# Products of a constant bf16 tile in 25 gaps of TensorE, in a fused four-layer network on one core

## The chip, the cores and the metric

One core of one Trainium2 chip runs one program. Its engines work side by side, each through its own list of instructions, and meet only at semaphores and barriers: TensorE (PE: matmuls and PE-mode transposes; PEld is its loading of weights), VectorE (DVE), ScalarE (ACT), GpSimd (POOL) and SyncE (SP, which issues most DMAs). The metric is the device time of one execution in microseconds (us), lower is better, as the median of several runs.

TensorE's clock has two levels here, 1.2 and 2.4 GHz. The profile shows what was granted as a share of the higher one: 0.50 is 1.2 GHz and 1.00 is 2.4 GHz.

## The reference

The residual stream x is [4, 256, 256] in float32, 1024 rows of 256. Four layers follow one another; each is an attention and a feed-forward part ("ffn"), each behind a layernorm and scaled by tanh of a gate:

```python
x = x + jnp.tanh(g_xattn[0]) * _L0_xattn_ref(_layernorm(x), ctx_512, ...)
x = x + jnp.tanh(g_ffn[0])   * _L0_ffn_ref(_layernorm(x), ...)
...
x = x + jnp.tanh(g_xattn[3]) * _L3_xattn_ref(_layernorm(x), ctx_512, ...)
x = x + jnp.tanh(g_ffn[3])   * _L3_ffn_ref(_layernorm(x), ...)
return x
```

What the parts compute:

```python
# layers 0 and 1: latent attention, 16 heads of 128, 64 latents per sequence (rope on
# the keys; in layer 0 on the queries too)
q_big  = jnp.einsum('bshk,hkq->bshq', (x @ Wq.T).reshape(B, S, H, K), w_kc_q)
scores = jnp.einsum('bhsr,bhlr->bhsl', q_r, k_r)
ctx_c  = jnp.einsum('bhsl,bld->bhsd', softmax(scores), kv_r)
out    = jnp.einsum('bhsd,hkd->bhsk', ctx_c, w_kc_kv) -> [B, S, H*K] @ Wo.T
# layers 2 and 3: causal attention with 16 heads of 16
scores = where(tril, q k^T / 4, min);  out = (softmax(scores) v) @ Wout.T
# ffn 0: top 6 of 16 experts (width 176) and one shared expert (width 352), silu gating
# ffn 1: w1, w2 made ternary by their mean size; gelu(x @ w1q.T + b1) @ w2q.T + b2
# ffn 2: rows of x and of the weight rounded to int8, one product, scaled back, + bias
# ffn 3: top 2 of 8 experts (width 512) and one shared expert, silu gating
```

## The kernel before

The whole stream stays in on-chip memory (tile X, 128 partitions by 8 token tiles of 256). The work is written out as a row of blocks, one for each part of a layer. A block lists each engine's instructions by hand; at its end all engines meet in a barrier, which each reaches only when its own work has drained. So no engine can start a part before the slowest of the part before has ended. Within a block the order on each engine is fixed by the code, and semaphores pass tiles between engines.

The blocks in order, with the stretch of the profiled span that they take:

- attn0, two blocks. The first (0 to 174 us, called `latent_rope` in the code) goes over 8 pairs of heads. Before the loop TensorE makes the first pair's query weights (`query_weights(0, True)`) and turns the first half of the normalised input with PE transposes (`turn_rows`); after the loop it turns the last two pairs' probabilities (`turn(NP - 2)`, `turn(NP - 1)`, line 680). The second block (to 215 us, `latent_out`) projects to the output.
- ffn0 (215 to 464 us, tiles `ffn_...`, lines 2174 and on): transposes, router logits, a count of the chosen rows, the list of rows for each of 63 work items (`index()`, line 2491), then the 63 items. Each item begins with a gather of its rows by GpSimd's indirect DMA (line 2220); TensorE turns them (line 2518) and multiplies (lines 2510, 2541).
- chain1 (465 to 519 us): the weights of layer 1's attention are folded; at its end TensorE transposes the normalised stream (line 222, the helper `normalise`).
- attn1 (519 to 594 us), ffn1 (594 to 642 us), attn2 (642 to 711 us), ffn2 (711 to 735 us), attn3 (735 to 804 us). attn2 and attn3 run the same code (`plain_attend`): projections, then a loop over 8 token tiles with `turn` (line 1219), `context` (line 1230), `turn_context` (line 1238) and `project` (line 1244).
- ffn3 (804 us to the end): 16 transposes (line 1962), 32 router products of 8 columns (line 1970), then the shared expert in 8 items and the routed ones in 23 (`up` line 1994, `down` line 2021, `turn_h` line 2011).

Most float32 products are made of three: the helper `mm3` (lines 95 to 97) multiplies high and low halves of both operands in the type fp32r. ffn0's and ffn3's experts use plain float32. A "transpose" is a product with the identity.

## Time and profile before

| what | value |
|---|---|
| median of 3 runs (lowest, highest) | 1020.25 us (1019.51, 1020.53) |
| profiled execution, its own time | 1013.3 us |
| span of its instructions | 1011.5 us |
| mean granted TensorE clock over the span | 0.924 |
| TensorE busy | 887.4 us, 88% of the span |
| VectorE, GpSimd, ScalarE busy | 569.6, 424.9, 345.8 us |
| DMA | 84.81 MB, mean 84 GB/s |

The stretches in which the profile grants half the clock are, in us from the span's start: 167 to 181, 215 to 232, 236 to 239, 253 to 270, 468 to 471, 505 to 522, 584 to 587, 594 to 604, 642 to 649, 662 to 666, 707 to 727, 731 to 744, 754 to 758, 802 to 819, and from 1007 on. Clock records begin at 20.6 us; ahead of that the page shows full clock for want of a record.

How to read the rows further down: a timeline row has the start of an instruction (or of a run of equal ones, with their count behind the x), the time it took, its engine, its line in the kernel, the tile written and the tiles read, and in brackets how long the engine had idled before it and what released it. "PEq" or "SPq" there is an engine's sequencer, which is what a barrier looks like.

### The profile page before, as it was taken

To read this page: it belongs to the slowest core of one execution; us is meant where nothing else is said; L and a number is where in the kernel's file an instruction comes from. 1 tells how busy PE (TensorE), PEld (TensorE's weight loads), DVE (VectorE), ACT (ScalarE), POOL (GpSimd) and SP (SyncE) were. 2 spreads that over 40 slices of the span, in tenths; PEclk is the share of its full clock that TensorE was granted. 3 is DMA by queue.
4 is the path that set the end of the run, shared out by engine and by line. 5 is a ranking of instruction groups with operands and counts; after the bars stand their busy time and mean duration, and the time that the engine had idled before them with its cause. 6 is when DMAs were issued, how large, how long until landed. Compare 5 with 4: busy or idle time off the path is not lost. (4 is left out here: it accounts for less than half of the span.)

```text
span 1011.5 us, 14571 instructions
## 1 busy us (share of the span) xinstructions
PE 887.4 (88%) x4711; PEld 690.1 (68%) x4711; DVE 569.6 (56%) x1068; ACT 345.8 (34%) x612; POOL 424.9 (42%) x341
## 2 busy tenths in 40 slices
PE   4999995988699999999859978897389799999996
PEld 3899995986466666667649966776278665566564
DVE  5788886549344344443578977667767532222221
ACT  3454543311133333333425436333143421122111
POOL 5787883030388888674402230630360006122222
PEclk9999998978699999999969979899579879999999
DMA  8321110039445435756520010100000194322210
GB/s 304 128 78 56 45 44 1 1 123 409 132 81 85 79 69 87 149 74 177 155 84 1 1 37 1 38 1 1 11 0 1 51 427 172 86 45 43 36 30 11
DMA packets 38593, 84.81 MB, mean 84 GB/s; under 512 B 9741, under 2 KB 27533, under 8 KB 36014
## 3 DMA queue, kind: packets, MB, share of 16 engines
q1 hardware_dynamic: 22062, 64.56, 18.1%
q0 software_dynamic: 16176, 19.31, 11.5%
q8 instruction: 39, 0.64, 0.3%
q14 instruction: 28, 0.23, 0.1%
q10 hardware_dynamic: 288, 0.07, 0.0%
HBM read 71.23 MB, written 20.68 MB: 91 GB/s over the span
## 5 line engine op out<-in xcount | busy, mean ns | idle before, releaser
L2510 PE MATMUL ffn_GU<-ffn_W,ffn_XTB 128*128 x252 | 91.2, 484 | 1.9 <-DVE ffn_XTB L2418 1.3
L1994 PE MATMUL ffn_GU<-ffn_W,ffn_XTB 128*128 x184 | 85.0, 604 | 0.0
L2220 POOL DMA_INDIRECT kept_MARKED<-scratch_rows,kept_IDX x63 | 62.4, 990 | 51.5 <-DMA scratch_rows<-ffn_WEIGHT 32.6
L1815 POOL DMA_INDIRECT out_x<-ffn_YB,ffn_XB x23 | 35.8, 1557 | 113.5 <-DVE ffn_YB L1943 92.3
L2402 DVE TENSOR_TENSOR ffn_GB<-ffn_GU,ffn_BIAS 128x352 f32<-128x352 f32 x63 | 33.0, 524 | 88.2 <-PE ffn_GU L2510 88.2
L2510 PEld LDWEIGHTS ffn_GU<-ffn_W,ffn_XTB 128*128 128x128 f32 x252 | 43.7, 191 | 34.3 <-issue 20.1
L2541 PE MATMUL ffn_DN<-ffn_W,ffn_HT 96*128 x252 | 64.8, 379 | 0.0
L2258 ACT ACTIVATE ffn_HG<-ffn_GB 128x176 f32<-128x176 f32 x63 | 22.1, 350 | 115.6 <-DVE ffn_GB L2402 115.6
L2021 PE MATMUL ffn_DN<-ffn_W,ffn_HT 128*128 (+1 forms) x248 | 58.7, 380 | 0.8 <-ACT ffn_HT L1838 0.8
L1932 DVE COPY ffn_XTB<-ffn_XP 128x256 f32<-128x256 f32 x23 | 9.8, 424 | 87.6 <-PE ffn_XP L2003 87.6
L1994 PEld LDWEIGHTS ffn_GU<-ffn_W,ffn_XTB 128*128 128x128 f32 x184 | 33.1, 189 | 36.0 <-issue 33.7
L348 POOL TENSOR_TENSOR attn_RP<-attn_RP,attn_RS 128x512 f32<-128x512 f32 x32 | 40.6, 1291 | 34.3 <-DVE attn_RS L515 34.3
L2021 PEld LDWEIGHTS ffn_DN<-ffn_W,ffn_HT 128*128 128x128 f32 x248 | 45.2, 190 | 9.2 <-issue 4.4
L1832 ACT ACTIVATE ffn_HG<-ffn_GU 128x512 f32<-128x512 f32 x31 | 18.5, 597 | 90.9 <-PE ffn_GU L1994 90.9
L2541 PEld LDWEIGHTS ffn_DN<-ffn_W,ffn_HT 96*128 96x128 f32 x252 | 43.0, 190 | 3.5
L343 POOL TENSOR_TENSOR attn_WS_lo<-attn_W,attn_WS_hi 128x896 fp32r<-128x896 f32 (+2 forms) x24 | 41.4, 1742 | 5.4 <-ACT attn_WS_hi L419 5.4
L95 PE MATMUL attn_QB<-attn_XT_hi,attn_C_hi 128*128 128x512 f32 x96 | 39.2, 408 | 3.0 <-DVE attn_XT_lo L557 3.0
L1062 POOL TENSOR_TENSOR attn_PROB<-XN,attn_SM 128x1024 f32<-128x1024 f32 x8 | 15.2, 1904 | 62.6 <-DVE attn_SM L1085 62.6
L97 PE MATMUL attn_QB<-attn_XT_hi,attn_C_lo 128*128 128x512 f32 x96 | 38.0, 396 | 0.0
L96 PE MATMUL attn_QB<-attn_XT_lo,attn_C_hi 128*128 128x512 f32 x96 | 38.0, 396 | 0.0
L1838 ACT ACTIVATE ffn_HT<-ffn_HP 128x512 f32<-128x512 f32 x31 | 18.5, 597 | 55.1 <-PE ffn_HP L2011 55.1
L1926 DVE TENSOR_TENSOR ffn_HF<-ffn_GU,ffn_HG 128x512 f32<-128x512 f32 x31 | 21.4, 691 | 25.9 <-ACT ffn_HG L1832 25.8
(506 smaller groups left out, 2471.3 us busy)
## 6 DMA issues: line engine op xcount, KB each, us to landing
ffn_W<-in_f_w SPq DMA_DIRECT2D x9, 1536.0 KB, 19.3
ffn_W<-in_f_w SPq DMA_DIRECT2D x16, 608.0 KB, 17.6
attn_W<-in_L_pairs SPq DMA_DIRECT2D x7, 1088.0 KB, 4.9
scratch_rows<-in_rows_empty SPq DMA_DIRECT2D x1, 2967.0 KB, 13.3
ffn_XB<-scratch_rows SPq DMA_DIRECT2D x23, 129.0 KB, 2.1
ffn_BIAS<-in_f_bias SPq DMA_DIRECT2D x1, 2816.0 KB, 16.4
kept_STAGE<-in_f_w SPq DMA_DIRECT2D x1, 2048.0 KB, 7.9
kept_STAGE<-in_L_pairs SPq DMA_DIRECT2D x2, 768.0 KB, 9.1
```

The lines of the kernel that those rows point to most:

```text
L95: pe.matmul(out, a[0], b[0], start=first, stop=False)
L96: pe.matmul(out, a[0], b[1], start=False, stop=False)
L97: return pe.matmul(out, a[1], b[0], start=False, stop=last)
L343: pool.tensor_tensor(WS[1][:, SECTIONS[c]], W[:, SECTIONS[c]], WS[0][:, SECTIONS[c]].bitcast(F32), ALU.subtract).then_inc(w_lo[c], 1)
L348: pool.tensor_tensor(RP[:, q, g, :], RP[:, q, g, :], RS[:, g, 1 - q, :], ALU.add).then_inc(rope_add, 1)
L1815: pool.indirect_dma_start(out[:, :], bass.IndirectOffsetOnAxis(ap=XB[:, i % NB, D:D + 1].bitcast(I32), axis=0), YB[:, i % 3, :], None, bou ...
L1994: last = pe.matmul(GU[:, m, :], x, weights(e, k * 2 * HID3 + m * HID3, HID3), start=k == 0, stop=k == KD - 1)
L2021: last = pe.matmul(DN[:, n % 2, 0:D], HT[:, n % 2, c * P:(c + 1) * P], weights(e, UPW + c * D, D), start=c == 0, stop=c == HID3 // P - 1)
L2220: pool.indirect_dma_start(XB[:, i % NB, :], None, DR["rows0"][:, :], bass.IndirectOffsetOnAxis(ap=IDX[:, i:i + 1], axis=0)).then_inc(rows_ ...
L2402: dve.tensor_tensor(GB[:, n % 2, :], GU[:, n % 2, 0:2 * HID], BIAS[:, bass.ds(e * (2 * HID), 2 * HID)], ALU.add).then_inc(biased, 1)
L2510: last = pe.matmul(GU[:, n % 2, 0:2 * HID], XTB[:, i % 2, k * P:(k + 1) * P], flat[:, bass.ds(e * WIDTH0 + k * 2 * HID, 2 * HID)], start=k ...
L2541: last = pe.matmul(DN[:, n % 2, 0:D], HT[0:rows, n % 2, j * P:(j + 1) * P], w, start=j == 0, stop=j == len(parts) - 1)
```

## The change

A tile WARM of 128 by 512 bf16 values is added and set to 1.0 by VectorE, as its first memset. A helper `keep_busy(pe, bank, n)` issues n products of WARM's first 128 columns with all of WARM into a PSUM bank that nobody reads at that point. Nothing else is computed with it. It is called at 25 places, 311 products in all. The numbers, in program order: attn0 9, 18, 4, 24 and 7; its second block 7; ffn0 5, 7 and 32; chain1 46; attn1 6 and 5; ffn1 8, 6, 8 and 14; attn2 8, 8 and 5; ffn2 24, 12 and 20; attn3 8, 8 and 12. ffn3 gets none. Three waits come with them: PE waits for the memset before the first group, in chain1 for 14 of 16 halves before the 46, and in ffn2 for one step of scaling before the 20. In attn1 the wait for the eighth shift stands ahead of the 6.

```diff
         MASK = sbuf(top, "CAUSAL", [P, L], BF16)
+        WARM = sbuf(top, "WARM", [P, 512], BF16)
...
             xt[:] = split(ctx, "XT", [P, KD, B * S])
+
+        def keep_busy(pe, bank, n):
+
+            for _ in range(n):
+                pe.matmul(bank, WARM[:, 0:P], WARM[:, :], start=True, stop=True)
...
-            def tensor(pe):
+            def tensor(pe, between=None):
                 for j in range(4):
+                    if j == 2 and between:
+                        between()
                     if j // 2 >= normalised:
...
                 x_in = [sem(ctx, f"x_in_{h}") for h in range(2)]
-                consts_set, mask_steps, gates_done, kvb_cleared = (sem(ctx, s) for s in ("consts_set", "mask_steps", "gates_done", "kvb_cleared"))
+                consts_set, mask_steps, gates_done, kvb_cleared, warm_set = (sem(ctx, s) for s in ("consts_set", "mask_steps", "gates_done", "kvb_cleared", "warm_set"))
                 rope, kvb_ready = Count(sem(ctx, "rope_steps")), sem(ctx, "kvb_ready")
...
+                        dve.memset(WARM[:, :], 1.0).then_inc(warm_set, 1)
                         for part in KVB:
...
+                        pe.wait_ge(warm_set, 1)
+                        keep_busy(pe, TR[:, 1, :], 9)
                         query_weights(0, True)
+                        keep_busy(pe, TR[:, 1, :], 18)
                         turn_rows(0)
                         turn_rows(1)
+                        keep_busy(pe, TR[:, 1, :], 4)
...
                         turn(NP - 2, False)
+                        keep_busy(pe, QB[:, 0, :], 24)
                         turn(NP - 1, False)
+                        keep_busy(pe, QB[:, 0, :], 7)
...
                                 last.then_inc(out_ps, 1)
+                        keep_busy(pe, ZP[:, 0, :], 7)
...
                             step(g)
+                        pe.wait_ge(g_lo, 4 * ROUNDS - 2)
+                        keep_busy(pe, GB[:, 0, :], 46)
                         pe.wait_ge(g_lo, 4 * ROUNDS)
...
                                 value(2 * i)
+                            if i == T:
+                                pe.wait_ge(shifted, T)
+                                keep_busy(pe, SC[:, 0, :], 6)
                             if 1 <= i <= T:
...
                                 mix(i - 2)
+                        keep_busy(pe, SC[:, 0, :], 5)
...
                         score(1)
+                        keep_busy(pe, TR[:, 0, :], 8)
                         for i in range(1, STEPS):
...
                                 turn(i - 1)
+                            if i == STEPS - 1:
+                                keep_busy(pe, TR[:, 0, :], 8)
                             if i >= 2:
...
                                 context(i - 1)
+                        keep_busy(pe, TR[:, 0, :], 5 if following else 12)
...
                         pe.matmul(UP[:, 0, 0:2], ONES[:, :], ASUM[:, 1:4:2], start=False, stop=True).then_inc(mean_ps, 1)
-                        nrm["tensor"](pe)
+                        nrm["tensor"](pe, lambda: keep_busy(pe, UP[:, 3, :], 8))
+                        keep_busy(pe, UP[:, 3, :], 6)
...
                                 pe.wait_ge(nrm["ready"], 4)
+                                keep_busy(pe, NB[:, 3, :], 8)
                             pe.wait_ge(h_lo, NF * (t // 4 + 1))
...
                                 up(n)
+                        keep_busy(pe, UP[:, 0, :], 14)
...
                         last.then_inc(wt_ps, 1)
+                        keep_busy(pe, OP[:, 0, :], 24)
                         turn_tokens(0)
+                        keep_busy(pe, OP[:, 0, :], 12)
                         turn_tokens(1)
...
                             last.then_inc(out_ps, 1)
+                        pe.wait_ge(scaled_steps, 1)
+                        keep_busy(pe, SP[:, :], 20)
...
                         for j in range(4):
+                            if j == 2:
+                                keep_busy(pe, RL[:, :], 5)
                             if j // 2 == 1:
...
                         def count():
+                            keep_busy(pe, RL[:, :], 7)
                             pe.wait_ge(chosen, 1)
...
                         index()
+                        keep_busy(pe, XP[:, :], 32)
                         pe.wait_ge(w_in, 16 * E)
```

Line numbers of the changed kernel are higher than those of the one before, by 9 near the start and by 33 in ffn3. Its order of instructions shows the new products as rows of line 153. Three places follow.

TensorE at the start of attn0; the rows of attn_WS are the query weights of pair 0, the row with IDENT is `turn_rows(0)` and `turn_rows(1)`. Before:

```order
L97 MATMUL attn_QB<-attn_WS_hi,attn_WS_lo 128x192
L603 MATMUL attn_QB<-IDENT,XN 128x128 x8
L95 MATMUL attn_QB<-attn_XT_hi,attn_C_hi 128x512
L96 MATMUL attn_QB<-attn_XT_lo,attn_C_hi 128x512
L97 MATMUL attn_QB<-attn_XT_hi,attn_C_lo 128x512
```

And in the changed kernel:

```order
L97 MATMUL attn_QB<-attn_WS_hi,attn_WS_lo 128x192
L153 MATMUL attn_TR<-WARM 128x512 x18
L612 MATMUL attn_QB<-IDENT,XN 128x128 x8
L153 MATMUL attn_TR<-WARM 128x512 x4
L95 MATMUL attn_QB<-attn_XT_hi,attn_C_hi 128x512
L96 MATMUL attn_QB<-attn_XT_lo,attn_C_hi 128x512
L97 MATMUL attn_QB<-attn_XT_hi,attn_C_lo 128x512
```

Eighteen products now stand between the weights and the transposes, and four between the transposes and the queries.

TensorE in ffn0, from the last step of `index()` to the first item (the row with ffn_TURNED ends the index, TENSOR_LOAD reads the item's expert number, the row with kept_MARKED turns the gathered rows), in the changed kernel:

```order
L2523 MATMUL ffn_RA<-IDENT,ffn_OWN 1x128
L2527 MATMUL ffn_RL<-ffn_TURNED 128x63
L153 MATMUL ffn_XP<-WARM 128x512 x32
L2581 TENSOR_LOAD ffn_EI
L2581 ISA x2
L2554 MATMUL ffn_XP<-IDENT,kept_MARKED 128x128 x2
```

Only the row of WARM is new; the 32 products stand ahead of the load and of the wait for the gathered rows.

TensorE at the end of attn3 (attn_CT is `context`, attn_OP<-IDENT is `turn_context`, the next row `project`, the branches are the block's end, and the last row is the first of ffn3). Before:

```order
L1230 MATMUL attn_CT<-kept_VB,attn_AT 128x34 x8
L1238 MATMUL attn_OP<-IDENT,attn_CN 128x128 x2
L1244 MATMUL attn_OP<-ffn_QO,attn_CTS 128x256 x2
L1162 UNCONDITIONAL_BRANCH
L1956 UNCONDITIONAL_BRANCH
L1962 MATMUL ffn_GU<-IDENT,ffn_XE 128x128 x8
```

And in the changed kernel:

```order
L1252 MATMUL attn_CT<-kept_VB,attn_AT 128x34 x8
L153 MATMUL attn_TR<-WARM 128x512 x8
L1260 MATMUL attn_OP<-IDENT,attn_CN 128x128 x2
L1266 MATMUL attn_OP<-ffn_QO,attn_CTS 128x256 x2
L153 MATMUL attn_TR<-WARM 128x512 x12
L1184 UNCONDITIONAL_BRANCH
L1989 UNCONDITIONAL_BRANCH
L1995 MATMUL ffn_GU<-IDENT,ffn_XE 128x128 x8
```

Eight products now stand between the last context and its transposes, and twelve between the last projection and the barrier.

## Rows read from the trace of the kernel before

**Rows 1.** TensorE's timeline, 0 to 24 us: start, us, engine, line, op, tiles, [idle <-releaser]

```profile
7.87 0.53 PE L95 MATMUL attn_QB<-attn_WS_hi 128*128 128x192 f32 x1 [7.87 <-POOL attn_WS_lo L343]
...
14.31 1.94 PE L603 MATMUL attn_QB<-IDENT,XN 128*128 128x128 f32 x8 [3.56 <-DVE XN L552]
...
19.11 0.63 PE L95 MATMUL attn_QB<-attn_XT_hi,attn_C_hi 128*128 128x512 f32 x1
19.53 0.63 PE L96 MATMUL attn_QB<-attn_XT_lo,attn_C_hi 128*128 128x512 f32 x1
...
21.19 0.40 PE L95 MATMUL attn_QB<-attn_XT_hi,attn_C_hi 128*128 128x512 f32 x1
21.43 0.39 PE L96 MATMUL attn_QB<-attn_XT_lo,attn_C_hi 128*128 128x512 f32 x1
...
23.13 1.04 PE L603 MATMUL attn_ST<-IDENT,XN 128*128 128x128 f32 x8
```

**Rows 2.** Stretches: length; busy us of PE, PEld, DVE, ACT, POOL; clock; DMA share; GB/s

```profile
249.31:252.72 3.41, 3.41 (x58) 3.41 (x58) 3.10 (x13) 0.00 (x0) 0.00 (x0) 1.00 1.02 415
252.72:256.13 3.41, 2.11 (x20) 1.23 (x18) 1.32 (x5) 0.00 (x0) 0.00 (x0) 0.50 1.02 411
723.76:727.18 3.42, 2.82 (x18) 2.28 (x19) 2.99 (x5) 1.02 (x1) 2.80 (x1) 0.50 0.02 5
727.18:730.59 3.41, 1.05 (x8) 0.49 (x6) 2.18 (x8) 0.00 (x0) 3.39 (x6) 1.00 0.00 0
```

**Rows 3.** The same view of eight stretches at half clock

```profile
176.29:181.04 4.75, 4.75 (x22) 4.75 (x23) 1.38 (x2) 1.73 (x3) 0.00 (x0) 0.50 0.00 0
519.35:522.38 3.03, 3.03 (x7) 2.46 (x8) 0.00 (x0) 0.00 (x0) 0.00 (x0) 0.50 0.74 205
583.82:587.23 3.41, 3.41 (x19) 3.41 (x18) 1.23 (x1) 2.60 (x3) 0.00 (x0) 0.50 0.02 5
642.07:648.67 6.60, 6.60 (x30) 6.38 (x31) 2.88 (x7) 3.05 (x8) 3.54 (x4) 0.50 0.27 78
708.07:711.31 3.24, 2.76 (x6) 1.46 (x6) 0.00 (x0) 0.38 (x1) 0.00 (x0) 0.50 0.00 0
735.02:744.24 9.22, 9.22 (x38) 8.60 (x39) 5.81 (x15) 5.23 (x14) 5.44 (x6) 0.50 0.00 0
754.65:757.90 3.25, 3.25 (x12) 2.71 (x12) 1.23 (x1) 1.24 (x2) 0.00 (x0) 0.50 0.00 0
804.14:819.34 15.20, 15.20 (x54) 12.32 (x55) 5.32 (x15) 4.02 (x5) 0.33 (x2) 0.50 0.92 366
```

**Rows 4.** TensorE's timeline at gaps that receive products

```profile
171.67 1.97 PE L680 MATMUL attn_TR<-IDENT,XN 128*128 128x128 f32 x8 [6.28 <-POOL XN L358]
...
264.60 0.69 PE L2518 MATMUL ffn_XP<-IDENT,kept_MARKED 128*128 128x128 f32 x2 [7.22 <-DMA kept_MARKED<-scratch_rows,kept_IDX]
...
514.03 3.64 PE L222 MATMUL chain_GB<-IDENT,XN 128*128 128x128 f32 x16 [12.83 <-DVE XN L197]
...
642.07 0.55 PE L95 MATMUL attn_TR<-kept_CWS_hi 64*128 64x256 f32 x1 [3.88 <-PEq L126]
...
798.92 0.44 PE L1238 MATMUL attn_OP<-IDENT,attn_CN 128*128 128x128 f32 x2 [0.81 <-DVE attn_CN L1350]
799.84 1.13 PE L1244 MATMUL attn_OP<-ffn_QO,attn_CTS 128*128 128x256 f32 x4 [0.47 <-ACT attn_CTS L1292]
```

**Rows 5.** TensorE's timeline, start of the last layer's experts

```profile
804.14 1.97 PE L1962 MATMUL ffn_GU<-IDENT,ffn_XE 128*128 128x128 f32 x8 [3.17 <-DVE ffn_XE L1855]
...
807.61 6.83 PE L1970 MATMUL ffn_LG<-ffn_RW,XN 128*128 128x8 f32 x32
...
814.29 6.18 PE L1994 MATMUL ffn_GU<-ffn_W,XN 128*128 128x512 f32 x8
...
822.45 3.60 PE L1994 MATMUL ffn_GU<-ffn_W,XN 128*128 128x512 f32 x8
```

**Rows 6.** VectorE's timeline, its last work of attn3

```profile
801.99 0.18 DVE L153 BATCH_NORM_AGGREGATE MOM<-STATS 128x2 f32<-128x6 f32 x1
```

## The prediction

> **What bounds the kernel now.** I read three views in this order: the granted clock over the span, the busy time of each engine in chosen stretches, and TensorE's timeline around its gaps. TensorE is busy 88% of the span, so most of the program is its chain; but the mean granted clock is 0.924, which makes (1 − 0.924) / 0.5 x 1011.5 = 154 us at half clock, in some fifteen stretches, and TensorE works in only part of them. The question is where its half-clock work stands at the end of a wait. What the level costs is in the rows: the starts of two 512-column fp32r products lie 0.42 us apart early in the program and 0.24 us apart two microseconds later, and 8 transposes take 1.94 and then 1.04 us [rows 1]; 8 plain float32 products take 6.18 and then 3.60 us [rows 5]. All else in such a stretch stays as it is.
>
> The half-clock stretches in which TensorE works without a pause, or almost, are these, with its busy time: 4.75 us behind attn0, 3.03 at the start of attn1, 3.41 near its end, 6.60 at the start of attn2, 2.76 at its end, 9.22 at the start of attn3, 3.25 at its first `turn` and 15.20 at the start of ffn3 [rows 3]. Together 48.2 us of work, which would take half, so 24 us is about what better clock could give in them if nothing else bound there. In each the clock was low because TensorE had stood still just before: 6.28 us ahead of L680, 12.83 ahead of L222, 3.88 ahead of attn2 [rows 4], 3.17 ahead of ffn3 [rows 5].
>
> **Do bf16 products lift the clock?** Nearly all of the kernel's own work is float32. But in ffn2, 723.76 to 727.18, TensorE ran 18 bf16 transposes and products for 2.82 us at half clock, and the next stretch had full clock [rows 2]. So bf16 work counts. Narrow work did not: in 249.31 to 252.72 58 products, most of 16 columns, kept TensorE busy for all of the stretch, and the clock fell behind it [rows 2]. WARM's products are 512 columns wide, as the float32 ones behind which it rose at 20 us and at 819, so I expect them to hold or lift it. Their price has no row; a bf16 product of 512 columns I take as one fp32r product of that width, 0.24 us at full and 0.42 us at half clock [rows 1], from nearest rows. Below that it could hardly be, since the operand streams as many columns; above it would be the plain float32 price, 3.60 / 8 = 0.45 us at full clock [rows 5].
>
> **Part by part**, + for time gained:
>
> 1. Start of attn0. Nine products start at once and even at 0.42 us (3.8 us) end within the 7.87 us of the first wait [rows 1]. The 18 have 3.56 us ahead of the transposes [rows 1]: 7.6 us at half clock, 4.3 at full. I expect a mix that delays the transposes by about 1.2 us. Then 8 transposes take 0.9 us less, and half of the first dozen queries some 0.2 us less each: +2. Net +0.8, between −2 (all cold) and +1.7.
> 2. End of attn0. 24 products at 0.24 are 5.8 us, within the 6.28 us before L680 [rows 4], which then costs 1.04 instead of 1.97: +0.9. Behind it 4.75 us of work at full clock [rows 3]: +2.1, since the first product of a block still loads its weights alone. Together +3.0. The 7 at the block's end fit in the wait behind it.
> 3. Second block's end. VectorE's last work there is the same residual add and statistics as at the end of attn3, where it ends 802.17 [rows 6] and TensorE 800.97 [rows 4], so 1.2 us of cover. 7 products are 1.7: −0.5.
> 4. ffn0. The 5 and 7 lie in a part paced by the loading of weights and end well ahead of the gather. The 32 fill the 7.22 us wait for the gathered rows [rows 4]; they begin at half clock. With ten at 0.42 and 22 at 0.24 they end after 9.5 us, 2.3 us late. What follows, transposes and the first item's products, ran at half clock until 269.8 and gets about 2.5 us back: +0.2, between −4 and +1.3.
> 5. chain1. 46 products are 11.0 us of a 12.83 us gap [rows 4], and they start at full clock. 16 transposes of 3.64 us [rows 4] gain 1.0 (VectorE's normalising paces the rest) and 3.03 us of attn1's first products [rows 3] gain 1.5: +2.5.
> 6. End of attn1: 3.41 us of dense work [rows 3] gains 1.5. ffn1's start waits on VectorE for its ternary weights: 0.
> 7. ffn1's end. 14 products are 3.3 us, TensorE's own work ends at 642.07 − 3.88 = 638.19 [rows 4]; with 1.2 us of cover as in 3: −2.0 (0 if VectorE's tail is longer).
> 8. Start of attn2: 6.60 us [rows 3], of which ScalarE's and VectorE's copies pace a part: +2.7. First `turn`, same code as attn3's: +1.6. Its end: 2.76 us [rows 3], +1.2.
> 9. Start of attn3: 9.22 us with VectorE busy 5.81 and ScalarE 5.23 [rows 3], so they can follow, not everywhere: +3.4. First `turn`, 3.25 us: +1.6. ffn2 itself is paced by VectorE and GpSimd: 0.
> 10. End of attn3. 8 products, 1.9 us, go into a 0.81 us gap [rows 4]: −1.0. 12 products, 2.9 us, start at 799.84 + 1.13 = 800.97 [rows 4] and end at 803.8, where VectorE is done at 802.17 [rows 6]: −1.6.
> 11. Start of ffn3: 15.20 us with no gap. The two groups of transposes gain 1.9, the 32 logits 3.4 if their weight loading follows the clock (6.83 [rows 5]), the first `up` 2.6 (6.18 to 3.60). That is 7.9. Against it: the logits are 8 columns wide, and behind such work the clock fell in ffn0 [rows 2]; then 3.4 us of `up` run at half speed, 1.7 lost. I take +6.0. What follows is TensorE's chain to the end, and GpSimd's scatter and the row loads follow the same chain, so the gain stays.
>
> Sum: 0.8+3.0−0.5+0.2+2.5+1.5−2.0+5.5+5.0−2.6+6.0 = 19.4 us. The profiled execution took 1013.3 us, 1.8 more than its span; it would take 993.9. The median of the runs is 7.0 us above the profiled one, so I forecast 1020.25 − 19.4 = 1000.9.
>
> **A page's rule.** In rows 5 TensorE did 16 transposes without a pause from 804.14 to 807.6, and the clock stayed at half [rows 3]. The Trainium skill, "TensorE: Matmul & The Clock Gate", Part 4 (PE-mode transpose), says that full clock does not engage in transpose mode, since it does not count as busy in the same way. The trace agrees so far as that stretch goes, but cannot tell a transpose from work that began too late. By that rule the products buy ffn3 little; it is the second rival.
>
> **Rivals.**
>
> - The gain is taken by other engines. At the starts of attn2, attn3 and ffn3 TensorE's output passes through VectorE or ScalarE; if these pace, gains shrink: 2.0 behind attn0, 1.8 in chain1, 0.8 at attn1's end, 1.5+0.8+0.6 in attn2, 2.0+0.8 in attn3, 4.5 in ffn3, together 14.8, less the costs 5.1: about 10, so 1010. For it: XT's halves are copied by both before the first queries. Against: in 735.02 to 744.24 TensorE had no pause at all [rows 3]. Chance 15%.
> - The clock does not hold over transposes. ffn3 would gain only its first group, 2 instead of 6; chain1 loses 1.0, and the two first `turn`s, attn3's start and attn0's end some 2 together: 19.4 − 7 = 12.4, so 1008. For it: rows 5 as above, and the narrow rows 2. Against: loops of heads have many transposes and keep full clock. Chance 15%.
> - Slower: the products neither lift nor hold the clock, as constant operands switch nothing. Then each costs 0.42 us: 24 need 10.1 us of 6.28 (+3.8), 46 need 19.3 of 12.83 (+6.5), 32 need 13.4 of 7.22 (+6.2), 18 need 7.6 of 3.56 (+4.0), 12 need 5.0 of 1.2 (+3.8), 14 need 5.9 of 1.2 (+4.7), 20, 12 and 24 in ffn2 about 7, and the rest of ten small groups 1 to 2 each, 12: about 48, so 1068. It decides from the point where a group at half clock is longer than its gap, which nine of the groups are. Chance 4%; the bf16 row in ffn2 speaks against it. Were only half the groups cold, the sum would be near zero: 4% for within 0.2%.
> - That the change doesn't do what it says, TensorE standing still just behind each group long enough for the clock to fall at once, is the same 1020, and in that 4%.
>
> **How the numbers follow.** The forecast has 62%, with its own range 995 to 1006. Costs of attn0, ffn0 and ends of blocks together hold ±4, the clock in ffn3 ±2. With both slower gains the range reaches 1012; downwards full clock through ffn3 and short overruns give 27, 993. A measurement of this kernel can tell 0.2%, 2 us. Faster 0.92 (the forecast and the first two rivals), within 0.2% 0.04, slower 0.04.
>
> **What would show it.** Full clock in the stretches of rows 3 apart from a part of ffn3's; L680 at 1.04 us; attn3's first products at 0.24 us from start to start; ffn3's 16 transposes at about 2.1 us together, logits about 3.5, first `up` between 3.6 and 5.5. Rows of the new line 153 at 0.24 us apart, and at 0.42 only in the first group and the first third of the 32. ffn3's first transpose some 1.6 us further behind the last projection than before. Wrong would be WARM products with half clock behind them, or transposes and logits in ffn3 as slow as before; or a wait of TensorE for VectorE in attn3's first 9 us as long as the gain.

## The result and the profile after

| | before | changed |
|---|---|---|
| median of 7 runs each (lowest, highest) | 1020.53 us (1019.51, 1024.11) | 1009.51 us (1008.78, 1015.28) |
| profiled execution: own time, span | 1013.3, 1011.5 us | 1009.2, 1007.4 us |
| mean granted clock over the span | 0.924 | 0.967 |

The ratio is 0.9905, with a 95% interval of 0.988 to 0.9931: 1.0% faster, 9.7 us by the ratio and 11.0 between the medians. The forecast of 1000.9 us had the sign and the mechanism, but nearly twice the size. The changed kernel was run twice more beside before: 1000.67 against 1012.63 us (0.9886, 0.9855 to 0.9916) and 1011.34 against 1019.48 us (0.991, 0.9878 to 0.9943). These are other chips; the ratios agree, the absolute times do not, so a kernel's median is given beside that of before in its own series, and traces are compared stage by stage.

The head of the page of the changed kernel (section 1's shares, then the granted clock in 40 slices):

```profile
span 1007.4 us, 15178 instructions
...
PE 933.2 (93%) x5006; PEld 696.5 (69%) x5022; DVE 571.2 (57%) x1069; ACT 345.4 (34%) x612; POOL 424.3 (42%) x341
...
PEclk9999999987899999999989999999999899999999
```

TensorE is busier by 45.8 us: 72.9 us of WARM's products less 27.1 us that the rest got shorter. Five slices still show less than full clock. The time of half clock went from 154 us to (1 − 0.967) / 0.5 x 1007.4 = 66 us. By the two traces TensorE was busy in 99.0 us of the first and in 54.2 us of the second, 8.4 of them WARM's. So nearly 90 us more of full clock, over half of it above TensorE's own work, bought 11 us; the account of the three pairs of traces below shows where the rest went.

What the groups cost and what stood behind them (TensorE's timeline of the changed kernel; the products of WARM are the bf16 rows of line 153; a count is short where a record is missing):

```profile
10.25 5.67 PE L153 MATMUL attn_TR<-WARM 128*128 128x512 bf16 x18
15.76 1.04 PE L612 MATMUL attn_QB<-IDENT,XN 128*128 128x128 f32 x8
...
164.78 5.13 PE L153 MATMUL attn_QB<-WARM 128*128 128x512 bf16 x23
171.02 1.09 PE L689 MATMUL attn_TR<-IDENT,XN 128*128 128x128 f32 x8 [1.11 <-POOL XN L366]
171.95 1.67 PE L153 MATMUL attn_QB<-WARM 128*128 128x512 bf16 x7
174.76 0.36 PE L95 MATMUL attn_out_ZP<-attn_Y_hi,KVB_hi 128*128 128x256 f32 x1 [1.14 <-PEq L325]
```

Against [rows 1]: the 18 products at the start of attn0 took 5.67 us, between 18 x 0.216 = 3.9 at full and 7.7 at half clock, so the clock rose under them, and the 8 transposes behind take 1.04 instead of 1.94 us. Against [rows 4]: the 24 products fill the old wait of 6.28 us (5.13 for the 23 recorded, 0.216 us each from start to start), L689, which was L680, takes 1.09 instead of 1.97 us, and the next block has full clock. This place went as forecast. The same view of the changed kernel in ffn0, where the first item begins:

```profile
256.87 8.04 PE L153 MATMUL ffn_XP<-WARM 128*128 128x512 bf16 x31 [0.22 <-issue]
264.75 0.38 PE L2554 MATMUL ffn_XP<-IDENT,kept_MARKED 128*128 128x128 f32 x2
```

Against the 7.22 us wait in [rows 4]: item 0 begins behind the 32 products, 3.4 us later than the gathered rows would have let it (experiment 3 has the working). The same view around the start of ffn3:

```profile
788.96 3.05 PE L153 MATMUL attn_TR<-WARM 128*128 128x512 bf16 x7 [0.22 <-issue]
...
793.68 2.75 PE L153 MATMUL attn_TR<-WARM 128*128 128x512 bf16 x12
798.38 1.82 PE L1995 MATMUL ffn_GU<-IDENT,ffn_XE 128*128 128x128 f32 x8 [1.95 <-DVE ffn_XE L1888]
800.00 1.92 PE L1995 MATMUL ffn_DN<-IDENT,ffn_XE 128*128 128x128 f32 x8
801.70 3.78 PE L2003 MATMUL ffn_LG<-ffn_RW,XN 128*128 128x8 f32 x32
805.34 5.38 PE L2027 MATMUL ffn_GU<-ffn_W,XN 128*128 128x512 f32 x8
```

Against [rows 5]: the 12 products end at 796.4, the transposes begin 1.95 us later, at half clock (1.82 and 1.92 us for 8); the router products take 3.78 instead of 6.83 us, the first `up` 5.38 instead of 6.18. And 44 us on, in the shared experts:

```profile
849.44 3.48 PE L2054 MATMUL ffn_DN<-ffn_W,ffn_HT 128*128 128x256 f32 x8 [4.87 <-issue]
```

This is a stall of 4.87 us, for which the profile names no cause ("issue"): TensorE waited for a copy of ScalarE that started 7.6 us after its input was done. Before's first trace has none. At ffn3's first `turn_h` this execution was 9.8 us ahead, at its end 4.1.

**Where the time came from.** I give the lead of each block's first TensorE instruction over the same instruction of before, as a gain per stage, for three pairs of traces: A the two on record, B and C the second and third trace of each kernel, both of a pair from one chip. A's two may be from different chips: the profiled execution of before took 1013.3 us, less than any of its seven timed runs (1019.51 and more), and as much as on the chip of B.

| stage | forecast | A | B | C | mean |
|---|---|---|---|---|---|
| attn0, first block | +1.7 | +1.5 | +3.0 | +4.0 | +2.8 |
| attn0, second block | +1.6 | +1.8 | +1.9 | +1.1 | +1.6 |
| ffn0 | +0.2 | −2.8 | +3.1 | −0.5 | −0.1 |
| chain1 | +1.0 | −0.3 | +0.2 | −0.5 | −0.2 |
| attn1 | +3.0 | +1.5 | +1.2 | −0.1 | +0.9 |
| ffn1 | −2.0 | −1.4 | −1.5 | +0.1 | −0.9 |
| attn2 | +5.5 | +5.4 | +3.3 | +3.2 | +3.9 |
| ffn2 | 0 | −0.7 | −2.0 | −0.7 | −1.1 |
| attn3 | +2.4 | +0.8 | +2.3 | +2.5 | +1.9 |
| ffn3 to the first `turn_h` | +6.0 | +4.0 | +2.2 | +2.9 | +3.0 |
| the rest of ffn3 | 0 | −5.7 | −0.2 | −2.8 | −2.9 |

Without the last line the means sum to 11.8 us; the medians show 11.0, 12.0 and 8.1. The last line is the stall; experiments 12 and 15 are about it. So the shortfall of 7.6 us against 19.4 has its parts in ffn3 (−3.0), attn1 (−2.1), attn2 (−1.6), chain1 (−1.2) and ffn2 (−1.1), with attn0 and ffn1 better by 1 each.

The same leads can be taken apart by what TensorE did up to ffn3's first `turn_h`: its own work (busy time without line 153), the products added, and its idle time:

| us | A | B | C |
|---|---|---|---|
| own work, shorter by | 28.9 | 31.4 | 28.7 |
| products of WARM, added | 72.9 | 72.6 | 73.2 |
| idle time, shorter by | 53.8 | 54.9 | 56.4 |
| lead | 9.8 | 13.7 | 11.9 |

TensorE's own work got shorter by 30 us. The products took 73 us and removed only 54 to 56 us of idling; the difference of 17 to 19 us is products that outlasted their gaps, and own work whose place a wait took.

### The profile page after: what moved, and what is told of

The parts are those of the page before. It is cut to its first block and busy times, and to the rows that moved or that the text cites. A ratio compares the mean times of both kernels' runs of the same rounds, so it can differ in the third digit from the quotient of the medians.

```text
span 1007.4 us, 15178 instructions
## 1 busy us (share of the span) xinstructions
PE 933.2 (93%) x5006; PEld 696.5 (69%) x5022; DVE 571.2 (57%) x1069; ACT 345.4 (34%) x612; POOL 424.3 (42%) x341
## 5 line engine op out<-in xcount | busy, mean ns | idle before, releaser
L1084 POOL TENSOR_TENSOR attn_PROB<-XN,attn_SM 128x1024 f32<-128x1024 f32 x8 | 15.2, 1904 | 61.3 <-DVE attn_SM L1107 61.3
```

## The experiments

**1 and 2. Both kernels again.** No edit.

> The kernel before, unchanged, for a second trace. Its median stood 7 us above its profiled execution; the changed kernel's median stood 0.3 us above its own, whose trace has one stall of 4.9 us in TensorE's idle time put down to nothing (ffn_DN at 849.4 us, with ScalarE's copy ahead of it 7.7 us late). Theory A (such stalls belong to most executions of either kernel, and the first trace of before missed them): this trace shows stalls of that kind worth 5 to 7 us in the shared or routed experts of ffn3, the span is near 1018. Theory B (the stall is made by the change): no such stall, span 1011 to 1012 and the 7 us stay unexplained. Either way the part ahead of ffn3's experts repeats the first trace within 0.5 us at each block's start.

Median 1011.78 us beside 1012.63 for the same kernel as reference (0.9991, 0.9976 to 1.0006); span 1012.1, no stall. That is what theory B said of this trace, but the whole series is 8 us quicker here than in the result, so it decides nothing between the two. The block starts did not repeat within 0.5 us: they are 0.3 to 1.0 us later than in the first trace.

> The changed kernel, unchanged, for a second trace. Whatever is fixed by the program repeats: ffn0's first item at 265 us with TensorE in WARM products until the gathered rows have long landed, attn3's end about 3.7 us later than its lead before it, WARM products 0.216 us apart at full and 0.427 at half clock. What hangs on where the clock falls may differ by 1 to 2 us a place. Theory A: the stall in ffn3 is there again or in a like place. Theory B (it is chance in this kernel): gone, span near 1002.

Median 1000.67, span 998.6. No stall in ffn3, as theory B had it. ffn0's first item did not repeat: 260.06 instead of 264.75 us. Two rows tell why: in this trace the index was ready early, and the 32 products ended ahead of the gathered rows (TensorE's timeline of again_after):

```profile
250.86 8.41 PE L153 MATMUL ffn_XP<-WARM 128*128 128x512 bf16 x32
260.06 0.44 PE L2554 MATMUL ffn_XP<-IDENT,kept_MARKED 128*128 128x128 f32 x2 [0.78 <-DMA kept_MARKED<-scratch_rows,kept_IDX]
```

What did repeat was the place that I had put at nothing, the end of ffn2. VectorE's last row there and TensorE's:

```profile
723.65 0.18 DVE L159 BATCH_NORM_AGGREGATE MOM<-STATS 128x2 f32<-128x6 f32 x1
```

```profile
719.02 7.25 PE L153 MATMUL ffn_SP<-WARM 128*128 128x512 bf16 x20
726.57 0.35 PE L95 MATMUL attn_TR<-kept_CWS_hi 64*128 64x256 f32 x1 [0.30 <-PEq L1644]
```

The 20 products stand behind a wait of 2.38 us, take 7.25 us (0.363 each: most at half clock) and end at 726.3; VectorE was done at 723.8. All engines wait 2.4 us for products that compute nothing. In A the same group took 6.1 us and ended 1.2 us late. And TensorE's timeline of the same trace in ffn3:

```profile
793.26 1.09 PE L1995 MATMUL ffn_GU<-IDENT,ffn_XE 128*128 128x128 f32 x8 [1.95 <-DVE ffn_XE L1888]
794.76 1.09 PE L1995 MATMUL ffn_DN<-IDENT,ffn_XE 128*128 128x128 f32 x8 [0.41 <-DVE ffn_XE L1888]
795.69 3.64 PE L2003 MATMUL ffn_LG<-ffn_RW,XN 128*128 128x8 f32 x32
800.94 6.46 PE L2027 MATMUL ffn_GU<-ffn_W,XN 128*128 128x512 f32 x8 [1.61 <-DMA ffn_W<-in_f_w]
```

Here transposes and router products all had full clock, and what they gained ran into a wait of 1.61 us for the shared expert's weights. Behind it the first `up` took 6.46 us. In [rows 5] there was no such wait, since the router products ended 12 us behind the block's start; here they end 7.7 us behind it, and the weights land at 800.9.

**3. A shorter group in ffn0.**

```diff
-                        keep_busy(pe, XP[:, :], 32)
+                        keep_busy(pe, XP[:, :], 12)
```

> Of the changed kernel, ffn0's group of 32 products behind the index is cut to 12. Theory 1 (the gather moved forward by 3.2 us with the blocks ahead of it, and the 32 products cover that lead): TensorE starts the first item at about 261.5 us instead of 264.9, all later blocks start 2.5 to 3.3 us earlier, the median is 3 us less, near 1006.5. Theory 2 (the items that follow are paced by the gathers or by the weights anyway): the lead shrinks away within ffn0, chain1 starts as before, median near 1009.5.

Median 1001.18 us beside 1000.67 (intervals 0.9851 to 0.9919 and 0.9855 to 0.9916): no difference, and neither theory as I wrote them. TensorE's timeline of gather12:

```profile
254.40 4.09 PE L153 MATMUL ffn_XP<-WARM 128*128 128x512 bf16 x12
260.16 0.44 PE L2554 MATMUL ffn_XP<-IDENT,kept_MARKED 128*128 128x128 f32 x2 [1.67 <-DMA kept_MARKED<-scratch_rows,kept_IDX]
```

Item 0 starts at 260.16, as with 32. But all seventeen traces of this study fit one rule: item 0 starts at the later of two times, the landing of a table that the gather needs (`scratch_rows<-ffn_WEIGHT`, which moves with the block's start) plus 4.0 us, and the end of the group. Landing to start is 264.60 − 260.62 in before, and again 4.1 and 4.0 in experiments 2 and 3. With 32 products the group takes 8.0 to 9.0 us. Where the index's last product ended by 252.9 us this cost 0.2 us or nothing; where it ended between 253.9 and 257.1 (five traces, A among them), item 0 came 2.4 to 3.5 us later than the landing allows. The index is later where the clock is down for longer around it (half clock from 246 to 259 us in A, from 247 to 254 in experiment 2). With 12 products the group was last in none of four traces, with indices that ended up to 257.1. So 32 is a risk of 3 us that pays nothing. That is read from the traces; the medians do not resolve it.

**4. attn3's groups moved into ffn3.**

```diff
-                                keep_busy(pe, TR[:, 0, :], 8)
+                                keep_busy(pe, TR[:, 0, :], 8 if following else 3)
...
-                        keep_busy(pe, TR[:, 0, :], 5 if following else 12)
+                        keep_busy(pe, TR[:, 0, :], 5 if following else 4)
...
                     def _(pe):
+                        keep_busy(pe, NBANK[3], 8)
                         for j in range(4):
```

> Of the changed kernel, the 12 products at attn3's end are cut to 4, 8 are put at the start of ffn3's list on TensorE (ahead of the wait for the normalised rows, in a bank that the fourth group of transposes overwrites later), and the 8 ahead of attn3's last transposes of the context are cut to 3. Theory 1 (the groups at attn3's end hold up the barrier, and the 1.95 us gap behind it lets the clock fall): barrier 1.9 us earlier, the last projection 1.1 to 2.5 us earlier, the first transposes of ffn3 at full clock (1.1 us for 8 instead of 1.8); together 4 to 6 us, median 1004 to 1005. Theory 2 (the clock in ffn3 falls by the transposes and narrow products whatever stands ahead): only the barrier's 2 to 3 us, logits or first up at half clock again, median about 1006.5.

Median 999.45 us beside 1000.67, not told apart (0.987, 0.9837 to 0.9903). TensorE's timeline of move_ffn3:

```profile
789.67 1.82 PE L153 MATMUL attn_TR<-WARM 128*128 128x512 bf16 x4
791.79 1.89 PE L153 MATMUL ffn_DN<-WARM 128*128 128x512 bf16 x8 [0.30 <-PEq L1184]
793.51 1.04 PE L1996 MATMUL ffn_GU<-IDENT,ffn_XE 128*128 128x128 f32 x8
794.94 1.09 PE L1996 MATMUL ffn_DN<-IDENT,ffn_XE 128*128 128x128 f32 x8 [0.39 <-DVE ffn_XE L1888]
795.87 4.80 PE L2004 MATMUL ffn_LG<-ffn_RW,XN 128*128 128x8 f32 x32
800.62 5.82 PE L2028 MATMUL ffn_GU<-ffn_W,XN 128*128 128x512 f32 x8
```

The gap of 1.95 us is filled and the transposes have full clock, yet router products (4.80) and first `up` (5.82) fall back, with products running until the first of them. ffn3's start to the first `turn_h` takes 14.4 us, 15.6 in the trace of experiment 2, 17.8 in before. attn3 itself takes 67.0 us, no less than in experiment 2 (66.7), because its own end now ran at half clock (4 products in 1.82 us). Of the 1.2 us that ffn3's start gained over experiment 2, 0.6 are an earlier start of `up` (the weights landed 0.6 us sooner behind the first transpose) and 0.6 lie behind it; the 16 transposes take 2.5 us here and took 2.6 there, with the gap. So filling the gap gave nothing that these two traces show, and nothing of theory 1's 4 to 6 us came; as theory 2 had it, router products and `up` are at half clock again.

**5. One group alone.** All groups set to nothing but the 12 at attn3's end.

> The changed kernel with all groups left out but the 12 products at the end of attn3. My sum said of this place: the barrier 1.6 us later, ffn3's start 6.0 us less, so 4.4 less in all, 1008.2 against 1012.6. The theory formed since (the wait for ffn3's weights, 9.4 us behind the block's start, takes the place of the half-clock work): transposes and logits gain over 5 us, but the first up starts only 9.4 us behind a block that starts 1.5 us later, at half clock again: 1.5 us less in all, or 3.5 if it runs at full clock; 1009 to 1011.

Median 1011.39 beside 1012.62 us (1.0005, 0.9979 to 1.0031), where my sum for this place promised 4.4 us. 4.4 us would be a ratio of 0.9957, outside that interval. TensorE's timeline of end12_only:

```profile
801.91 1.09 PE L1995 MATMUL ffn_GU<-IDENT,ffn_XE 128*128 128x128 f32 x8 [1.95 <-DVE ffn_XE L1888]
...
804.35 3.64 PE L2003 MATMUL ffn_LG<-ffn_RW,XN 128*128 128x8 f32 x32
808.94 6.70 PE L2027 MATMUL ffn_GU<-ffn_W,XN 128*128 128x512 f32 x8 [0.96 <-DMA ffn_W<-in_f_w]
```

attn3 takes 70.2 us instead of 69.0, ffn3's start to the first `turn_h` 15.2 instead of 17.8: 1.5 us in all. Router products 3.64, then 0.96 us of waiting for the weights, then 6.70 us for the first `up`. That is what the theory of the wait said; my term was wrong by 3 us.

**6 and 7. The wait for the weights.** First the order on SyncE:

```diff
+                        sp.dma_start(W[:, E, :], A["f3_w"][E]).then_inc(shared_in, 16)
                         sp.dma_start(RW[:, :, :], A["f3_router"]).then_inc(small_in, 16)
...
-                        sp.dma_start(W[:, E, :], A["f3_w"][E]).then_inc(shared_in, 16)
```

> The changed kernel with one DMA moved: in ffn3 the shared expert's weights are issued ahead of four small loads instead of behind five. In the second trace TensorE ended the router products at 799.3 and then stood 1.6 us for these weights, and ran the first up at half clock behind that. Theory 1 (the transfer is what is late next once transposes and logits are quick): weights land about 2 us earlier, the wait goes, up begins 1.6 us earlier and part of it at full clock; 1.6 to 4 us less, 997 to 999. Theory 2 (the router's small loads are then late instead, or the transfer shares its bandwidth with the eight that follow and lands no earlier): no gain, 1000.7.

Median 1005.0 us (0.994, 0.9919 to 0.996), beside 1012.62 for before, where the changed kernel had 1000.67 beside 1012.63. The edit puts the transfer ahead of all five small loads, and four of them are awaited before the router products. They were late (TensorE's timeline of w_first):

```profile
795.77 1.09 PE L1995 MATMUL ffn_DN<-IDENT,ffn_XE 128*128 128x128 f32 x8 [0.41 <-DVE ffn_XE L1888]
799.79 6.20 PE L2003 MATMUL ffn_LG<-ffn_RW,XN 128*128 128x8 f32 x32 [2.93 <-DMA ffn_COUNTUP<-in_count_up]
805.84 6.21 PE L2027 MATMUL ffn_GU<-ffn_W,XN 128*128 128x512 f32 x8
```

The router products waited 2.93 us for them, and behind that wait ran at half clock: 6.20 us for the 32 and 6.21 for the first `up`. The weights did land sooner, at 799.0, so theory 1 had the transfer right and theory 2 the result. The router products read one of the four loads but wait for all; that one alone ahead of the transfer was not tried, nor an issue of the transfer ahead of the barrier.

Then a wait that keeps the experts' weights behind the shared ones' landing:

```diff
+                        sp.wait_ge(shared_in, 16)
                         for e in range(E):
                             sp.dma_start(W[:, e, :], A["f3_w"][e]).then_inc(w_in, 16)
```

> The changed kernel with one wait on SyncE in ffn3: the eight experts' weights are issued only when the shared expert's have landed. In the changed kernel's second trace these landed 7.1 us behind their issue, those behind them 3.7 us apart, so the first shares its way. Theory 1 (the transfer binds the first up): it lands 1.0 to 1.4 us earlier, at 5.7 to 6.1 us behind the issue, the first up begins that much earlier and perhaps at full clock; 1 to 3 us less than 1000.7, 998 to 999.7. Theory 2 (no sharing, 7.1 us is the transfer's own latency): same landing, and the experts' weights about 5 us later, still well before their first use: no change.

0.9897 of before on its chip (0.9861 to 0.9934). From issue to landing 6.95 us, against 6.2 to 7.1 in other traces: the transfer landed no earlier by being alone, as theory 2 had it. In this trace it did not bind: the router products ran at half clock and ended at 805.9, the weights had landed at 803.3.

**8. chain1's group made longer.**

```diff
-                        keep_busy(pe, GB[:, 0, :], 46)
+                        keep_busy(pe, GB[:, 0, :], 54)
```

> Of the changed kernel, chain1's 46 products are raised to 54, so that they end 0.4 us instead of 2.2 us before the normalised rows. My term for this place was +2.5; traces show 1.4 and 0.4, with half clock in one or two stretches behind the gap. Theory 1 (the gaps of 2.2 and 1.7 us behind the group let the clock fall): transposes and the first products of attn1 at full clock, 1 to 1.5 us less up to the first softmax of attn1. Theory 2 (the clock falls by the transposes and the 1.7 us wait at the block's barrier): nothing, 1000.7.

0.9895 of before (0.9851 to 0.9939), as the changed kernel. TensorE's timeline of chain54 says more:

```profile
512.95 1.06 PE L230 MATMUL chain_GB<-IDENT,XN 128*128 128x128 f32 x8
514.37 1.09 PE L230 MATMUL chain_GB<-IDENT,XN 128*128 128x128 f32 x8 [0.35 <-DVE XN L203]
517.30 0.47 PE L95 MATMUL attn_SC<-chain_GS_hi,layer_XT_hi 128*128 128x512 f32 x1 [1.84 <-PEq L828]
517.61 0.40 PE L96 MATMUL attn_SC<-chain_GS_lo,layer_XT_hi 128*128 128x512 f32 x1
...
518.39 0.63 PE L96 MATMUL attn_SC<-chain_GS_lo,layer_XT_hi 128*128 128x512 f32 x1
```

Both groups of transposes have full clock (1.06 and 1.09 us), and so have the first products of attn1; then the clock falls under them (0.40 us, then 0.63 for one product). Behind these transposes stood gaps of 0.35 and 1.84 us. Closing the gap ahead of them moved the fall by some microseconds and did not avert it. chain1 takes 53.5 us in this trace, 54.7 to 54.8 in the three of the changed kernel and 54.0 to 56.4 in the others with 46 products: it may be worth up to 1 us, which one trace does not show and the medians do not resolve.

**9. ffn2's group made shorter.**

```diff
-                        keep_busy(pe, SP[:, :], 20)
+                        keep_busy(pe, SP[:, :], 11)
```

> Of the changed kernel, the 20 products at the end of ffn2 are cut to 11. In the second trace of the changed kernel (on the chip where before takes 1012.6 us) all 20 stood behind a 2.4 us gap, most ran at half clock, ended at 726.3 us, and VectorE had ended at 723.8. Theory 1 (an over-long group at half clock holds up the barrier by 2.4 us): attn3's block starts 2.0 to 2.4 us earlier against ffn2's last product, and what is lost by a later rise of the clock in attn3 is under 1 us; 1.5 to 2.3 us less, about 999 against 1000.7. Theory 2 (the clock in attn3's first stretch was what the 20 bought): attn3 starts at half clock and gives back 3 us; 1001 to 1002.

ffn2 takes 21.7 instead of 24.1 us by the traces (22.9 in the two other traces of the changed kernel), so the 1.2 to 2.4 us are real; attn3 gives 1.0 of them back. The span is 995.4, the lowest of all, but the median of 4 runs is 1002.07 (997.17 to 1003.78) beside 1012.62 for before, no better than the changed kernel's 1000.67 beside 1012.63: the time of whole runs, which scatter by several us, does not show it. Theory 1 for the stage, nothing shown for the whole.

**10. Together, with the moved transfer.** The edits of 3, 4, 8, 9 and the first of 6.

> All edits of the earlier and these kernels together: ffn0's 32 cut to 12, chain1's 46 raised to 54, ffn2's 20 cut to 11, attn3's last 8 cut to 3, its 12 at the end cut to 4 with 8 at ffn3's start, and ffn3's shared weights issued first. If each place gives what the traces show (ffn0 0 to 3, chain1 1, ffn2 2, attn3 2.4, weights 1.6 to 4) the sum is 7 to 10 us below the changed kernel, 991 to 994. If the clock falls elsewhere as the groups get shorter, about half: 996.

Median 1004.83 us (0.9914, 0.9888 to 0.994). ffn3's start repeats w_first (router products waiting 3.0 us) and takes 20.4 us, 4.8 more than in experiment 2. The others did not bring their sum either: at ffn3's first transpose this trace is 0.1 us ahead of experiment 2, with ffn2 2.4 us shorter and chain1 1.7 us longer, though its group was the longer one.

**11. Together, without it.** The edits of 3, 4 and 9, and the wait of 7.

> The changed kernel with ffn0's 32 cut to 12, ffn2's 20 to 11, attn3's last 8 to 3, its 12 at the end cut to 4 with 8 at ffn3's start, and the eight experts' weights issued behind the shared ones' landing. From the traces of the single edits: ffn2 2 us, attn3 and ffn3's start 1 to 2, weights 1 to 3, ffn0 0 to 3: 4 to 7 us below the changed kernel's 1000.7, so 994 to 997.

1004.50 beside 1021.91 us for before: 0.982 (0.9775 to 0.9866), and 7 us below chain54 and 6 below shared_alone in the same series. attn3 takes 64.7 us in its trace, the least of all.

**12. The stall and the chip.** Before, a third time.

> The kernel before, unchanged, a third trace. Three traces of changed kernels from chips on which before takes 1020 to 1022 us have a stall of 4.9 us in ffn3 about 40 us behind its start, four from a chip on which it takes 1012.6 have none, and so have both traces of before. Theory A (the stall belongs to the chip, not to the change): if this runs where before takes over 1018, its trace has a stall of about 5 us in the shared experts of ffn3 and a span near 1018; if it runs where before takes 1012 to 1013, it has none. Theory B (the changed kernels' shift in time makes it): none in either case.

Median 1021.28, so a chip of the other kind, and a stall in before too, though shorter than theory A's 5 us, with a span of 1015.4 (TensorE's timeline of third_before):

```profile
856.51 3.67 PE L2021 MATMUL ffn_DN<-ffn_W,ffn_HT 128*128 128x256 f32 x8 [2.56 <-issue]
```

**13 to 15. Eight products behind the router products.**

```diff
+                        keep_busy(pe, NBANK[3], 8)
                         pe.wait_ge(shared_in, 16)
```

> The changed kernel with 8 more products between ffn3's router products and the wait for the shared weights. In every trace so far the first up ran 5.4 to 6.8 us, near its half-clock time of 6.18, also where transposes and router products had full clock; behind the router products TensorE stands 0 to 1.6 us for the weights. Theory 1 (the narrow router products and the wait lower the clock just ahead of the first up): the 8 products take 1.7 us at full clock inside the wait, and the first up then has full clock in its second half at the latest: 4 to 5 us instead of 6; 1 to 2 us less than the changed kernel run beside it. Theory 2 (the clock is already lowered when the 8 begin): they take 3.4 us, the first up starts up to 2 us later and no quicker: 1 to 2 us more.

TensorE's timeline of logits8:

```profile
795.65 1.81 PE L1995 MATMUL ffn_GU<-IDENT,ffn_XE 128*128 128x128 f32 x8 [1.95 <-DVE ffn_XE L1888]
...
798.97 3.79 PE L2003 MATMUL ffn_LG<-ffn_RW,XN 128*128 128x8 f32 x32
802.61 3.53 PE L153 MATMUL ffn_DN<-WARM 128*128 128x512 bf16 x8
805.93 3.69 PE L2027 MATMUL ffn_GU<-ffn_W,XN 128*128 128x512 f32 x8
```

The 8 products ran at half clock (3.53 us), and behind them the first `up` ran at full clock for the first time, 3.69 us. So the clock is down when the router products end, though they took 3.79 us themselves, and somebody has to work at half clock until it rises; whether that is WARM or `up`, the first `turn_h` comes 15.5 us behind the block's start, against 14.9 in the trace beside it. 0.9909 (0.9871 to 0.9948) beside 0.991: no gain.

> As the best so far (ffn0 12, ffn2 11, attn3 3 and 4, 8 at ffn3's start), without the wait between the shared and the experts' weights, and with 8 products behind the router products. The best so far stood at 0.982 of before on its chip, the changed kernel at 0.989 to 0.9905. Expected 0.980 to 0.983; 0.985 if the 8 run at half clock.

0.9891 (0.9858 to 0.9924). The best so far is not confirmed: best2 differs from it by two edits that each moved nothing by themselves, and on this chip it is no better than the changed kernel. Its attn2 and attn3 took 67.6 and 66.9 us, where the best's took 65.3 and 64.7.

> The changed kernel, unchanged, beside these two on one chip. 0.9886 to 0.9905 of before. If before takes over 1018 us on this chip, a stall of 3 to 5 us in ffn3's shared experts; if 1012 to 1013, none.

0.991 (0.9878 to 0.9943). My label for the stall was too narrow: here nothing is put down to "issue", but ScalarE's copies are late again and TensorE waits 4.4 us for what follows from them. Better is the length of the stage, from the first to the last shared expert (first `turn_h` to the first routed row). It takes 39.0 to 39.4 us in all eight traces from chips on which before takes 1012.6 us, of either kernel, and 39.0 in the first trace of before, which fits such a chip by its 1013.3 us; it takes 43.1 us in third_before and 44.6 to 47.5 in the seven traces of changed kernels from the other chips. So it goes with the chip and is not made by the change alone, against theory B; whether the change makes it longer there (one trace of before against seven) stays open, and so does its cause. If the first trace of before is from a chip of the quicker kind, that explains the 7 us between its time and the median, which my forecast carried over unexplained; no record names its chip.

## Why the prediction was wrong

**The step that failed** is the sum of costs, and with it term 11. The gains that my terms give TensorE's own work add up to about 28 us, and 28.7 to 31.4 came. Against them I set costs of 1.2 (attn0), 0.5 (its second block), 2.3 (ffn0), 2.0 (ffn1) and 2.6 (attn3), together 8.6; measured, as what TensorE's own work got shorter in a stage less what the stage gained, they are 17.9 in the mean of the three pairs: 5.3 in ffn0, 3.6 in attn3, 3.1 in ffn2, where I had none, 2.9 in ffn1, 1.2 in attn0, 1.0 in ffn3 and 0.9 elsewhere. The mechanism, that these products hold and lift the clock, was right; the step from a clock gained to time gained was not.

**Right:** bf16 products of a constant hold and lift the clock (18 in attn0: 5.67 us, then 8 transposes in 1.04); their price (0.216 and 0.427 us, where I took 0.24 and 0.42); the groups of 24 in attn0 and 46 in chain1 fit their gaps; attn0 and its second block (+3.3 forecast, +4.4 measured); attn3's groups late at the barrier (I had 2.4 net for attn3, it gained 1.9). ffn1's end came out near (−2.0, measured −0.9) by luck: the cost was 2.9 us, and 1.9 us of own work that I had not counted came back. The third rival (constant products do nothing, 1068) is out.

**Wrong, by stage.**

1. Term 11, ffn3's start, 6.0 us, measured 3.0. I added the gains of transposes (1.9), router products (3.4) and first `up` (2.6) and took off 1.9. In the mean of the three pairs the transposes gave 0.7 (0.15 in A, at half clock; 1.0 in B and C, where at full clock the second group waited 0.4 us for VectorE), the router products 2.9, and all behind the start of `up` 0.1 instead of a net 0.7. A wait for the shared weights took 0.8 (0, 1.6 and 0.7). They land 6.2 to 7.1 us after an issue that follows the barrier, which no row of mine showed as a wait because TensorE had always been later. This is the question "what is late next" asked for copies and not for the transfer. And `up` never ran at full clock throughout: 5.4 to 6.8 us in every trace of a changed kernel but the two of logits8 and best2, where WARM paid instead. end12_only measured this term with its barrier cost at 1.5 against my 4.4.
2. Terms 5 and 6, chain1 and attn1, 4.0 us, measured 0.7. I took a full gap as enough for full clock behind it. The next gaps (2.2 us for the normalised rows, 1.7 for the barrier) stayed, and the clock fell in or behind them; chain54, which closed the first, only moved the fall. What [rows 3] shows for attn1's end (583.82 to 587.23) is moreover one execution's: in the second and third trace of before that stretch has full clock.
3. Term 8, attn2, 5.5, measured 3.9. In B it starts at half clock (636 to 643 us) despite 14 products 1.9 us ahead. In C there was less to gain: before's third trace has full clock at attn2's first `turn`, and its attn2 takes 68.5 instead of 70.8 us.
4. ffn2, 0, measured −1.1. I gave the 20 products no price, since VectorE and GpSimd pace the block. They do, but the group starts behind a wait of TensorE, partly at half clock, and outlasts both by 1.2 to 2.4 us.
5. Term 4, ffn0, forecast +0.2, measured −0.1 between −2.8 and +3.1: right in the mean by luck. A faster index bought nothing, since the table for the gather lands 45.1 to 45.4 us behind the block's first transpose in all six traces; and the 32 products made item 0 late by 3.4, 0.1 and 2.4 us. The items behind it took 197.3 to 197.5 us in the six traces of kernels with the groups on the quicker chips, against 200.1 for before there (my 2.5 us back), but 198.7 to 202.3 in the seven from the other chips.

Two rivals gave about the right size, the first (other engines take the gain, 1010) and the second (the clock does not hold, 1008), and neither for its reason. Of the first, ffn3's transposes bear out a small part, the 0.4 us for VectorE; but in attn2, where it took off most (2.6 us), TensorE's own work got 4.2 us shorter and the stage 3.9. The second has in its favour that the clock fell again in chain1, attn2 and ffn3. But its reason was transposes, and that is not what the traces show. The stretches around ffn3's start in the changed kernel, as in [rows 2]:

```profile
798.57:801.98 3.41, 3.41 (x18) 3.33 (x18) 1.98 (x6) 1.46 (x3) 0.33 (x2) 0.50 0.67 183
801.98:805.40 3.42, 3.42 (x32) 3.42 (x32) 0.66 (x1) 1.01 (x1) 0.00 (x0) 1.00 1.03 428
805.40:808.81 3.41, 3.41 (x5) 1.38 (x5) 2.52 (x8) 1.54 (x2) 0.00 (x0) 0.50 1.01 432
```

In the first of them 16 of the 18 instructions are transposes and the other two router products, in the second all 32 are router products of 8 columns. The clock rose behind the transposes and fell behind the router products, TensorE being busy all the time in both; in logits8 the same. In before the same transposes began behind a wait of 3.17 us and were followed at once by the router products, and the clock stayed down [rows 5]. The sentence of the Trainium skill, "TensorE: Matmul & The Clock Gate", Part 4 (PE-mode transpose), that full clock does not engage in transpose mode is contradicted by the first two rows, and by transposes that ran at full clock elsewhere (8 in 1.04 us at the start of attn0): the measurement decides.

## What to carry to other kernels

Work put into a gap to keep a clock must be sized by the price at half clock and by the engine that ends last at the next barrier; a group behind a wait, or at a block's end, is on the path at once when it outlasts either. A gain by a higher clock ends at the next transfer that is issued at a barrier: look for the landing, also where today nobody waits for it. Add up the costs as carefully as the gains: here the gain in TensorE's own work was forecast well, and the costs were double what was forecast. And where the clock level of a stretch changes from one execution to the next, a row at half clock is worth its gain times how often it occurs: attn1's end was at half clock in one of three traces of before.

## What the runs showed of the hardware

- A product of 128 by 128 with 512 columns in bf16 starts every 0.216 us at full and every 0.427 us at half clock; a run of such products of a constant lifts the clock, as the 18 did that took 5.67 us with the clock rising under them.
- 32 products of 8 columns, in float32, took 6.83 us at half clock and 3.64 at full, and their weight loads filled the stretch (PEld busy 3.42 of 3.42 us): the loading of weights follows the clock too. TensorE was busy with them all the time, and the clock fell behind them.
- Executions of one kernel differ in which stretches have half clock; the changed kernel's first item of ffn0 started at 264.8, 260.1 and 262.6 us in three traces.
- 1.5 MB from memory landed 6.2 to 7.1 us after their issue with eight such transfers behind them, and 6.95 and 6.56 us with none (shared_alone, best); put ahead of five small loads it made the four that the router products wait for 3 us late.
- Chips differ: before took 1012.6 us on two and 1019.5 to 1021.9 on the others. ffn3's shared experts took 39.0 to 39.4 us on the first kind; on the others 43.1 in the one trace of before and 44.6 to 47.5 in those of changed kernels, with late copies of ScalarE, whose cause no record names.
